# Softmax sums of four heads on GpSimd, turned gate logits, shorter fills, and a new plan

## The reference

```
x = x + 0.5 * ffn(layernorm(x))       # A
x = x + attention(layernorm(x))       # B
x = x + 0.5 * ffn(layernorm(x))       # C, same weights as A

ffn(x):  logits = x @ gate_w.T + gate_b        # 8 experts
         probs = softmax(logits); the two largest are kept
         h_e = relu(x @ w1[e] + b1[e])         # 128 -> 256
         out = sum over the two of probs_e * (h_e @ w2[e] + b2[e])
attention(x): q = x Wq.T, latent = x Wkv_down.T (64), k, v = latent Wk_up.T, latent Wv_up.T
         8 heads of 32; softmax(q k.T / sqrt(32)) v over the 512 tokens of the batch; then Wo
```

## Time and profile before

| | |
|---|---|
| median of 3 runs | 1193.15 us (1191.34 to 1196.9) |
| the profiled execution | 1193.1 us, its span 1191.3 us |
| TensorE busy | 1139.1 us, 96% |
| ScalarE busy | 912.3 us, 77% |
| VectorE busy | 721.9 us, 61% |
| GpSimd busy | 714.4 us, 60% |
| mean granted clock of TensorE | 0.970 |

### The profile page before, as it was taken

How to read it: one execution, slowest core, us unless ns; L and a number is a source line. 1 busy time by engine, 2 the same in 40 slices (tenths; PEclk the granted TensorE clock), 3 DMA queues, 4 the chain that set the end, 5 groups by cost and what they waited for, 6 DMA issues and landing times.

```text
span 1191.3 us, 26036 instructions
## 1 busy us (share of the span) xinstructions
PE 1139.1 (96%) x8278; PEld 759.2 (64%) x8278; DVE 721.9 (61%) x2254; ACT 912.3 (77%) x2255; POOL 714.4 (60%) x868
## 2 busy tenths in 40 slices
PE   7999998999999999999999999999999999999996
PEld 5677575676675557576666666666665456757675
DVE  4785568566785657375663676566657545647335
ACT  2348678678897989796898888888888887888431
POOL 3146568584848888028887653886701875268655
PEclk8998998999999999999999999999999889999988
DMA  8075573756645176656565636566732156548872
GB/s 287 1 251 167 176 224 110 243 159 204 203 136 149 47 227 210 177 149 183 178 210 154 181 123 183 161 206 196 211 107 63 41 159 178 148 148 249 257 257 73
DMA packets 159883, 202.07 MB, mean 170 GB/s; under 512 B 16938, under 2 KB 103426, under 8 KB 159747
## 3 DMA queue, kind: packets, MB, share of 16 engines
q1 hardware_dynamic: 144196, 168.90, 46.2%
q0 software_dynamic: 15360, 31.49, 9.1%
q10 hardware_dynamic: 192, 0.02, 0.0%
HBM read 152.50 MB, written 47.84 MB: 168 GB/s over the span
## 4 chain that ended last, share of the span: by engine, by line
PE 69%; POOL 10%; ACT 10%; issue 5%; DVE 3%; DMA 2%; SPq 0%; POOLq 0%; ACTq 0%; DVEq 0%
PE psum L1587 63%; ACT probs L1193 4%; ACT psum L1202 3%; POOL Y L1111 3%; POOL pause L1075 3%; PE psum L1707 2%; POOL slots_C L1091 2%; POOL slots_A L1091 2%; PE psum L1615 1%; PE psum L1772 1%; DVE neg_m L1541 1%; ACT hg L1239 1%; PE psum L1674 1%; DMA results_C<-ys 1%; ACT xnB L1158 1%
## 5 line engine op out<-in xcount | busy, mean ns | idle before, releaser
L1541 DVE TENSOR_REDUCE neg_m<-psum 128x1 f32<-128x512 f32 x512 | 317.6, 685 | 155.1 <-PE psum L1587 155.0
L1587 PE MATMUL psum<-nat 32*128 32x512 f32 x2048 | 364.4, 643 | 2.5 <-DVE ys L1521 1.4
L1202 ACT ACTIVATE psum<-psum,neg_m 128x512 f32<-128x512 f32 x512 | 341.6, 682 | 27.7 <-DVE neg_m L1541 26.9
L1193 ACT ACTIVATE probs<-psum 128x512 f32<-128x512 f32 x512 | 266.6, 630 | 43.2 <-PE psum L1587 41.6
L1587 PEld LDWEIGHTS psum<-nat 32*128 32x128 f32 x2048 | 130.6, 185 | 94.7 <-issue 24.3
L1075 POOL MEMSET pause<- 128x900 f32 x212 | 183.5, 866 | 0.1
L1587 PEld LDWEIGHTS psum<-xg_T,wt 128*128 128x128 f32 x1296 | 157.5, 195 | 40.2 <-ACT probs L1193 12.5
L1587 PE MATMUL psum<-xg_T,wt 128*128 128x128 f32 x1296 | 171.8, 283 | 5.3 <-DMA wt<-packed 3.5
L1587 PEld LDWEIGHTS psum<-wt,hg 128*128 128x128 f32 x1296 | 156.3, 196 | 31.6 <-ACT psum L1202 11.5
L1091 POOL DMA_INDIRECT slots_A<-xnA,posA x120 | 118.0, 983 | 95.0 <-DMA xs<-slots_A 44.9
L1587 PE MATMUL psum<-wt,hg 128*128 128x128 f32 x1296 | 166.7, 283 | 8.4 <-ACT psum L1202 3.7
(11 more groups left out here) (192 smaller groups left out, 1424.5 us busy)
## 6 DMA issues: line engine op xcount, KB each, us to landing
wt<-packed SPq DMA_DIRECT2D x324, 320.0 KB, 4.1
xs<-slots_A SPq DMA_DIRECT2D x36, 256.0 KB, 4.6
results_A<-ys SPq DMA_DIRECT2D x36, 256.0 KB
xs<-slots_C SPq DMA_DIRECT2D x36, 256.0 KB, 5.3
results_C<-ys SPq DMA_DIRECT2D x36, 256.0 KB
X<-in_L_attn_x_dram SPq DMA_DIRECT2D x16, 256.0 KB, 8.3
out_dram<-X SPq DMA_DIRECT2D x16, 256.0 KB
packed<-probs SPq DMA_DIRECT2D x1, 2560.0 KB, 8.2
```

Source lines behind the costliest of these rows:

```text
L1193: act.activation(probs[:, kt, j, :], at.banks()[j][:], ACT.Exp).then_inc(a_done, 1)
L1202: act.activation(at.banks()[j][:], at.banks()[j][:], ACT.Exp, bias=neg_m[:, g, n, j:j + 1], accum_out=sums[:, g, n, j:j + 1]).then_inc(S[" ...
L1541: V_.tensor_reduce(neg_m[:, g, n, j:j + 1], at.banks()[j][:], AX.X, ALU.max, negate=True).then_inc(S["r_done"], 1)
L1587: return nc.tensor.matmul(dst, w, m, start=start, stop=stop)
```

## The change

- `by_rows` returns True for the second four heads only (g = 1). The first four of each of the 16 batches take the other form: no exponential in place, and additions, products with ones, a reciprocal and a scaling instead.
- An addition on GpSimd is four instructions of 128 columns and not one of 512.
- The gate's weights stand still and the tokens move: `lgT` is four products of 32 stationary columns (8 real, the others zero) with 128 tokens each, in four column groups of one bank; ScalarE copies the 128x128 result to `lg_T`, and `logits` is one transpose of it. `lg_T` is there once, so a copy waits until the transpose before it is through.
- `KEEP` is gone, and with it all fill transposes.
- `pause` is two linked memsets of 150 columns; `GAP` is 2.95 and was 3.4.
- The tables that rank the tokens (24 selects on GpSimd) are made after the first normalised rows, not ahead of them.
- All wanted times are new, and some planned costs.

```diff
 def by_rows(b, g):
-    return True
+    return g == 1
...
-PERIOD, FIRST_B = 54.81, 448.4
+PERIOD, FIRST_B = 55.59, 661.63
...
-KEEP = {("B", 0, "xT", 0): 10, ("B", 2, "xT", 0): 2, ("B", 4, "mrow", 1): 2, ("B", 13, "mrow", 0): 1,
-        ("A", 0, "xTf", 0): 12, ("A", 6, "h", 0): 1, ("C", 8, "h", 4): 2, ("C", 11, "logits", 0): 1,
-        ("C", 10, "y", 1): 2, ("C", 12, "xTf", 0): 1}
-GAP = 3.4
+GAP = 2.95
...
-    "s": ((("PE", 1.28), ("ACT", 1.95)), 0.0), "pv": ((("PE", 3.7), ("ACT", 0.48)), 0.0), "add": ((("POOL", 1.27),), 0.0),
+    "s": ((("PE", 1.3), ("ACT", 1.95)), 0.0), "pv": ((("PE", 3.57), ("ACT", 0.48)), 0.0), "add": ((("POOL", 1.8),), 0.0),
...
-    "sum": ((("PE", 1.8), ("ACT", 0.96), ("DVE", 1.9)), 0.0), "wo": ((("PE", 1.85), ("DVE", 0.61)), 0.0),
-    "load": ((("SP", 0.48),), 4.0), "logits": ((("PE", 0.9), ("DVE", 0.15)), 0.0),
+    "sum": ((("PE", 1.85), ("ACT", 1.35), ("DVE", 2.3)), 0.0), "wo": ((("PE", 1.85), ("DVE", 0.61)), 0.0),
+    "load": ((("SP", 0.48),), 4.0), "lgT": ((("PE", 0.45), ("ACT", 0.28)), 0.0),
+    "logits": ((("PE", 0.17), ("DVE", 0.15)), 0.0),
...
-                pool.tensor_tensor(pairs[:, kt // 2, j, :], probs[:, kt - 1, j, :], probs[:, kt, j, :],
-                                   ALU.add).then_inc(S["p_added"], 1)
+                for n in range(TILES):
+                    last = pool.tensor_tensor(pairs[:, kt // 2, j, tokens(n)], probs[:, kt - 1, j, tokens(n)],
+                                              probs[:, kt, j, tokens(n)], ALU.add)
+                last.then_inc(S["p_added"], 1)
...
                 if at.step in after_pair:
-                    linked(pool.memset(pause[:], 0.0))
+                    for n in range(2):
+                        linked(pool.memset(pause[:, n, :], 0.0))
...
                 last.then_inc(S["rows_done"], 1)
+                if (s, b) == ("A", 0):
+                    rank_tables()
...
+            def lgT(at):
+
+                bank = a_bank(at)
+                i = lgT_order.index((at.stage, at.index))
+                if i:
+                    s0, b0 = lgT_order[i - 1]
+                    act.wait_ge(d_full, counts["d_full", (s0, b0, "logits", 0)])
+                act.activation(lg_T[:], bank[:, 0:P], ACT.Copy).then_inc(a_done, 1)
...
-                for _ in range(TILES * KEEP.get(at.step, 0) if not j else 0):
-                    nc.tensor.transpose(psum[bank][:, 0:P], ident[:], ident[:])
...
-            def logits(at):
+            def lgT(at):
                 bank = emptied_bank(at)
...
+                rows = P // TILES
                 for n in range(TILES):
-                    last = pe_mm(bank[:, n * EXPERTS:(n + 1) * EXPERTS], xT_F[:, i, tokens(n)], gw_T[:])
-                last.then_inc(d_full, 1)
+                    last = pe_mm(bank[n * rows:(n + 1) * rows, 0:P], gw_T[:], xT_F[:, i, tokens(n)])
+                last.then_inc(a_full, 1)
+
+            def logits(at):
+                bank = emptied_bank(at)
+                pe.wait_ge(a_done, at.count("a_done", "lgT", 0))
+                nc.tensor.transpose(bank[:, 0:P], lg_T[:], ident[:]).then_inc(d_full, 1)
```

More of the change, by code:

```diff
@@ L148, in wanted_experts @@
             at[s, b, "load", 0] = t - 12.0
-        for n, name in enumerate(("norm", "scaled", "xTf", "logits")):
+        for n, name in enumerate(("norm", "scaled", "xTf", "lgT", "logits")):
             at[s, b, name, 0] = t + 2.0 * n
@@ L202 @@
 D_STEPS = ("cen", "wqo", "wkv", "xT", "logits", "rank1", "rank2", "wo", "sum", "max", "dy", "y")
-A_STEPS = ("b2", "kv", "q", "k", "v", "s", "pv", "mrow", "h", "xg", "xTf", "dh")
+A_STEPS = ("b2", "kv", "lgT", "q", "k", "v", "s", "pv", "mrow", "h", "xg", "xTf", "dh")
 R_STEPS = ("rmax",)
@@ L338, in all_steps @@
             steps[s, b, "xTf", 0].takes.append("xTf_dense" if c == DENSE[s] else "xTf")
-            after((s, b, "logits", 0), (s, b, "xTf", 0), (s, b - 1, "logits", 0))
+            after((s, b, "lgT", 0), (s, b, "xTf", 0), (s, b - 1, "lgT", 0))
+            steps[s, b, "lgT", 0].takes.append("lgT")
+            after((s, b, "logits", 0), (s, b, "lgT", 0), (s, b - 1, "logits", 0))
+            steps[s, b, "logits", 0].gives.append((0, "lgT"))
             if c == DENSE[s]:
@@ L342, in all_steps @@
             else:
-                steps[s, b, "logits", 0].gives.append((0, "xTf"))
+                steps[s, b, "lgT", 0].gives.append((0, "xTf"))
             if b == FIRST[c]:
-                after((s, b, "logits", 0), (s, c - 1, "gate", 0), (s, c - 1, "top2", 0))
+                after((s, b, "lgT", 0), (s, c - 1, "gate", 0), (s, c - 1, "top2", 0))
             after((s, c, "top1", 0), (s, b, "logits", 0))
@@ L740, in macaron_kernel @@
     xTf_order = list(xTf_turn)
+    lgT_order = [st[:2] for st in order["PE"] if st[2] == "lgT"]
     routed = [st[:2] for st in order["DVE"] if st[2] == "top1"]
     scaled_steps = [st for st in order["DVE"] if st[2] == "scaled"]
-    first_steps = order["PE"][:order["PE"].index(("A", 0, "logits", 0))]
+    first_steps = order["PE"][:order["PE"].index(("A", 0, "lgT", 0))]
     assert all(bank != GATE_BANK for step in first_steps for bank, _ in order["banks"][step])
@@ L1303, in _ @@
             chain = Chain(dve, link)
+            chain(V_.memset(gw_T[:], 0.0))
             V_.memset(M[:, 0:EXPERTS], 0.0)
@@ L1599, in center_gate @@
                 pe.wait_ge(setup_dve, 2)
-                pe_mm(psum[GATE_BANK][:, EXPERTS:2 * EXPERTS], ones[:], gw_T[:]).then_inc(setup_pe, 1)
+                pe_mm(psum[GATE_BANK][:, EXPERTS:2 * EXPERTS], ones[:], gw_T[:, 0:EXPERTS]).then_inc(setup_pe, 1)
             def emptied_bank(at, j=0):
```

71 lines of the change are left out of this document (38 added, 33 removed), and 4 rows, old and new, of the table PARTS.

## The result

The changed kernel takes 1302.6 us (median of four, 1296.3 to 1306.4) beside 1195.0 for the kernel before on the same chip: a ratio of 1.0898, interval 1.0836 to 1.096. Forecast were 1172 us, with 1138 to 1212 as the range of eight in ten. The change is slower by 107.6 us.

What follows compares the result with a forecast made beforehand. TensorE, busy 96% of the span but partly held by waits for ScalarE, was taken as the bound. Terms -4.8 - 5 - 15 + 29.3 - 22 - 21 + 20 - 3 = -21.5 took 1193.1 to about 1172 us, range 1138 to 1212.

Steps and rivals of the forecast that it cites:

- Start: Kernel start: rank selects moved behind the first rows and fills dropped, transposes at 8.5 in place of 13.28 us; -4.8 us.
- Tail: GpSimd's closing chain of gathers from 1143.49 us: shorter filler memsets between pairs save 11 x 0.3; -3 us.
- Fills: TensorE's fill transposes: dropping the 48 not at the start or before the first attention batch; -5 us.
- Logits: The 32 logits steps on TensorE: four products in column groups plus one transpose replace eight instructions; -15 us.
- Sums by ones: Products with ones added to TensorE, 16 steps of 1.83 us; +29.3 us.
- ScalarE's relief: ScalarE loses 256 of 512 in-place exponentials and their reads; TensorE's waits for it shrink, -22 and -21 us.
- Additions on GpSimd: GpSimd's 128 additions of 1.76 us, late additions delaying ScalarE's `probs` by 1.25 us a batch; +20 us, ends 0 and 113.
- The handoff it priced: ScalarE may not write `probs` for heads 4 to 7 before GpSimd's last additions of heads 0 to 3; +20 us.
- the rival of the slow handoff: Late GpSimd additions make ScalarE, then TensorE, lose 4 us a batch: +64 in place of +20, 1216 us; chance 0.22.
- Clock: TensorE's granted clock: loss through the fills set at 0, with +10 us as the bad end.
- growing half-clock stretches: Sign in the new profile, TensorE's half-clock stretches growing, that would show the prediction wrong; no size given.
- Order: New shifts and planned costs on all engines: held at 0, with 10 us both ways in the range.

Runs made afterwards that it cites:

- b_nofill: The kernel before without its 136 fill transposes, every engine's order the same: ratio 1.0023.
- a_tinyadd: The changed kernel with GpSimd's additions of 4 columns in place of 128, same orders: 1204.0 us.
- b_tinyexp: The kernel before with ScalarE's in-place exponential on 8 columns in place of 512 for heads 0 to 3, same orders: time falls by 15 us.
- a_longpause: The changed kernel with the old GpSimd filler of 900 columns in place of two of 150, orders unchanged: 1278 us.
- a_tinyadd_fill: The changed kernel with additions of 4 columns and 416 fill transposes together: 1269 us.
- b_tables_few: The kernel before with rank tables behind the first rows and 16 first fill transposes in place of 48, long filler kept: ratio 0.9975.
- b_shortpause: The kernel before with GpSimd's filler as two linked memsets of 150 columns instead of one of 900, orders unchanged: +0.9%.
- b_short_few: The kernel before with the short filler and 16 first fill transposes in place of 48, rank tables early: 1289.8 us.
- a_fillgaps: The changed kernel with 416 fill transposes ahead of 38 steps where TensorE idled, same orders: 44 us faster than the changed kernel.

## Why the prediction was wrong, point by point

- *Start, Tail, Fills*: the first two happened as worked out (8.44 us; pairs 3.00 us apart, 3.1 forecast). The fills were worth 0 and not -5 (b_nofill: +0.2%). All three are small, and on this kernel they can't be had: fewer first fills and the short filler together cost 8%.
- *Logits*: mis-sized. The four products take 14.7/32 = 0.46 us a step where 0.23 was worked out, and the transpose 0.32 where 0.16 was. Together that is 0.78 against 32.8/32 = 1.02 before, so TensorE has 8 us less to do and not 17. What the term brings in time was not measured by itself.
- *Sums by ones*: 31.7/16 = 1.98 us a step, and 1.83 was forecast. The rest is the clock: 30.8/16 = 1.93 in a_tinyadd.
- *ScalarE's relief*: mis-sized. ScalarE has 774 us of work left and not 718, because the sum added up exponentials and accumulator reads (341.6 + 116.4 = 458.0) that overlap: together they occupied ScalarE for 357.7 us before and 178.4 after. Of the waits, the first half was read rightly: waits for the in-place exponential fell from 59.0 to 26.4 us, and VectorE's maxima are waited for 9.8. The second half, a third of 62.1 us of waits for ScalarE's other work, did not come: 43.0 and 18.3 are left of 43.2 and 18.9. And waits that go do not all turn into time: b_tinyexp gives 15 us for 90 off ScalarE, so about 23 for the change's 138, not 43.
- *Additions on GpSimd*: the step that failed most, +99 where +20 stood, and not by its own mechanism. Its sizes were right (462 ns a piece, 440 forecast; GpSimd 836 us busy, 848 forecast). The handoff it priced did not happen: nobody waits for the additions, which end 1.1 us or more ahead of the sums, and 1.7 us or more ahead of the next heads' `probs`, in every batch. So the rival of the slow handoff, 1216 us, is wrong as well; that it named the direction is luck. The range of this term, 0 to 113, held what came out; it was the range of the whole that was cut at 1212.
- *Clock*: 0, with +10 at the bad end, is the other step that failed. I asked only whether the clock would be lost through the fills. Half-clock time went from 71 to 175 us, which is at most 52 of the 107.6 us at half rate; the waits around it come on top. The text named growing half-clock stretches as a sign of failure; the sum had no term for what makes them grow.
- *Order*: +-10 was too narrow. After the relief (20 us less than forecast), the fills (5) and the sums (2), a_tinyadd is still 25 us over what my sum gives without the handoff. That rest holds the new order and the logits, not told apart. That a fixed order can shift by 97 us through two small edits shows how little +-10 was worth.
- *Why the additions cost the clock* stays partly open. Shown is one chain from beginning to end (streak of additions, VectorE held 11.0 us, TensorE out of work, half clock), and that it doesn't carry the whole: with linked pieces no VectorE operation is held, and the loss is as large. Shown is also that over the five forms of the additions the loss follows half-clock time and late products, and neither GpSimd's load nor what VectorE is held, and that 416 fills in TensorE's gaps took back 44 us. Over all versions half-clock time alone does not rank them: a_longpause has 169 us of it and is 25 us faster than the changed kernel with 175, a_tinyadd_fill has 79 and takes 1269. Not shown is what makes the products late, whether the falls of the clock or the late products cost more, which small delays end in a fall elsewhere, nor why fewer first fills, a difference of the first 14 us, matter to the end.

None of the versions that compute everything beats the kernel before by more than can be measured; the nearest is b_tables_few at 0.9975 [0.9945, 1.0004].

## What to carry to other kernels

Where TensorE is over 90% busy and its waits are short, price an edit by what it does to those waits and to the clock behind them, not by the work it moves; between additions of 64 and of 128 columns, 93 us more at half clock went with 95 us more of time. Additions on another engine that nobody waits for are not free for that. Look too at the waits for which the profile has no releaser: here they set the versions with the short filler apart from all others. On a kernel with a written-out order, try small edits together before you count them one by one, as two that measured +0.9% and -0.25% were +8% together, and leave the range open on the slow side.

## What the runs showed of the hardware

- A VectorE operation with two inputs in SBUF was held 11.0 us, through 32 GpSimd additions back to back that read SBUF; where each addition waited for the one before, none was held for over 0.5 us.
- Beside GpSimd's memsets of 900 columns, which read nothing, VectorE is held too. Casts, scalings and the like took up to 1.46 us over their median in the kernel before, 28 of them by over 0.5 us, 27.6 us together; with two linked memsets of 150 columns (b_shortpause) none was over 0.5. The kernel was 0.9% slower all the same.
- With the short memsets, beside an indirect DMA on GpSimd or within 2 us behind it, semaphores of TensorE came 1.0 us or more behind the shown end of their product (60 times in the changed kernel, up to 5.4 us; 67 times in b_short_few). With the long ones this was never seen in five versions and three times, in all of 3.6 us, in a_longpause.
- A GpSimd addition costs 202 ns at 4 columns, 322 at 64, 393 at 96, 462 at 128 and 1284 at 512: one long piece is 0.56 us cheaper than four short ones.
- With 55 us of fill transposes in gaps the mean clock was 0.976 in place of 0.933 (a_fillgaps), though late products were fewer as well; in the kernel before, leaving out all 136 left it at 0.971.
